# Weighting the edge one-hots on VectorE instead of GpSimd in a graph network kernel

## The chip, the cores and the metric

The kernel runs on one core of a Trainium2 chip. The metric is the device time of one execution in microseconds (us), from start to end, taken as the median of several executions. A profile of one execution gives, beside that, the span from the first to the last instruction and the start and length of every instruction.

## The reference

The program is a graph network on 1,250 nodes with 512 features. It first runs four layers of sparse attention and an MLP over 21,250 edges, then one last layer that sums neighbours with edge weights:

```python
scores = jnp.einsum('ehd,ehd->eh', q[src], k[dst])
...
out = jax.ops.segment_sum(attn[:, :, None] * v[dst], src, num_segments=N)
...
msgs = x[col] * vals[:, None]
agg = jax.ops.segment_sum(msgs, row, num_segments=n)
```

The kernel turns both sparse steps into dense ones. For that it needs two 1,250 x 1,250 tables: how many edges lead from node s to node d (the attention uses its logarithm), and the sum of the weights of those edges (the last layer multiplies by it).

## The kernel before

The work has three stages on the one core: the tables are built, then four layers run, then the last layer. The change touches the first stage alone.

**How the tables are built.** The edges are sorted by destination and cut into 56 groups of 384 (`GK` = 3 blocks of 128 edges each). A group's destinations lie within a window of `WIN` = 28 columns. For each group, TensorE multiplies the one-hots of the sources (`onehot`, 128 edges x 1280 nodes, bf16, one for each block) with a small operand `win` (128 edges x 4 x 28, bf16). The first of the four parts of `win` is the one-hot of the destination column in the window; the other three are that one-hot times the three bf16 parts of the edge's weight (`wpart`), which together hold the weight in full. The sums land in PSUM, and VectorE adds them into the tables `CW` in SBUF.

**Who does what in a group.** TensorE: 30 matmuls (L1464). VectorE: four additions into `CW` (L1060, L1062, L1064, L1067), of which the three on the weight table are a chain that must keep its order, and two of the source one-hots for the group three ahead (`sources`, L1028); for one group in eight it makes all three. ScalarE makes the third source one-hot of the other seven groups (L708, L770).

**The windows.** `win` is made for four groups at a time, a *chunk* (`CHUNK_G` = 4, so 14 chunks), in two alternating buffers. VectorE compares the column offsets (`window`, L1022: one TENSOR_TENSOR of 128 x 336 elements), and GpSimd then multiplies the result three times (L599: three TENSOR_TENSOR of 128 x 336 elements in a chunk). TensorE waits for `e_parts` before the first group of a chunk.

**Order.** The groups are run in blocks of eight (`groups(i)`, seven blocks). `j` is the group in the block. `window(1, ...)` stands at the end of group j = 0 and serves the groups j = 4 to 7 of the same block; `window(0, ...)` stands at the end of j = 4 and serves the next block. TensorE starts group n when VectorE has ended the chain of additions of group n - 2 (`e_chain`). Between blocks VectorE has other work (angles, remainders of the layers' rows, first statistics), and between chosen groups TensorE, ScalarE and GpSimd have some too (`between`). When the last group is added, VectorE sets `tables_done` (L1134), for which the other engines wait. All of this stands inside blocks that are entered when a flag says that the windows hold, which they do for these inputs.

## Time and profile before

| what | value |
|---|---|
| median of 3 runs | 1897.14 us (1895.46 to 1897.63) |
| profiled execution, its own time | 1893.53 us |
| span of that execution | 1891.7 us |
| granted TensorE clock, mean | 0.990 of full speed |
| TensorE busy over the span | 1765.5 us (93%) |
| VectorE busy | 1273.4 us (67%) |
| ScalarE busy | 915.1 us (48%) |
| GpSimd busy | 362.1 us (19%) |

The shares are averages over all stages. In the first 190 us, where the tables are built, the picture is another one than in the layers, and it has to be read by itself. In the rows of the trace, PE is TensorE, DVE is VectorE, ACT is ScalarE and POOL is GpSimd. The length of a VectorE instruction is from its start to its last write; the next one can start before that, so the distance between two starts tells what an instruction takes of the engine.

### The profile page before, as it was taken

How to read it: one execution, taken by the hardware profiler on the slowest of the kernel's cores; microseconds unless marked ns; L12 is line 12 of the kernel's file. 1: busy time of each engine (PE TensorE's matmuls, PEld its weight loads, DVE VectorE, ACT ScalarE, POOL GpSimd, SP SyncE). 2: the span in 40 equal slices, each digit the busy share in tenths (PEclk: the TensorE clock that was granted, in tenths of full speed). 3: DMA queues.
4: the chain of work that ended last, by engine and by line, in shares of the span. 5: the costliest groups of instructions: out<-in, count | busy, mean ns of one | idle time of the engine just before them, and what ended most of it. 6: DMA issues, size and time to landing. Idle time of an engine off the chain costs nothing.

```text
span 1891.7 us, 30938 instructions
## 1 busy us (share of the span) xinstructions
PE 1765.5 (93%) x11881; PEld 1510.1 (80%) x11881; DVE 1273.4 (67%) x2425; ACT 915.1 (48%) x1472; POOL 362.1 (19%) x482
## 2 busy tenths in 40 slices
PE   4755799999999999999999999999999999999898
PEld 3655588888887888888888888888878888888777
DVE  8999955766866566667655766767556667575744
ACT  8796744544542345445523544545325445453221
POOL 3222330000252200000532000004420000034201
PEclk9899999999999999999999999999999999999999
DMA  3040652422310223223200422323003223241121
GB/s 126 2 128 2 259 190 75 140 93 86 128 57 16 70 94 126 88 93 115 84 27 27 137 93 88 126 88 100 23 16 126 88 93 128 86 143 50 41 80 70
DMA packets 63926, 170.31 MB, mean 90 GB/s; under 512 B 5977, under 2 KB 24186, under 8 KB 63773
## 3 DMA queue, kind: packets, MB, share of 16 engines
q10 hardware_dynamic: 23040, 102.41, 16.2%
q1 hardware_dynamic: 40740, 65.91, 10.7%
q8 instruction: 96, 1.57, 0.3%
q14 instruction: 50, 0.41, 0.1%
HBM read 146.58 MB, written 17.02 MB: 86 GB/s over the span
## 4 chain that ended last, share of the span: by engine, by line
PE 77%; DVE 13%; issue 5%; ACT 2%; DMA 1%; DVEq 1%; POOL 1%; SPq 0%; POOLq 0%; ACTq 0%
PE ps L1464 66%; PE ps L1681 9%; DVE onehot L1028 2%; PE ps L1601 1%; DVE prob L1220 1%; DVE PT_lo L1236 1%; DVE CW L1062 1%; DVE CW L1064 1%; DVE CW L1060 1%; DVE CW L1067 1%; ACT PT_hi L835 1%; DMA piece<-in_L_gnn_m_w_dram 1%; DVEq L1052 1%; PE ps L1896 1%; DMA stacks_sb<-b_stack 0%
## 5 line engine op out<-in xcount | busy, mean ns | idle before, releaser
L835 ACT ACTIVATE PT_hi<-ps 128x512 fp32r<-128x512 f32 x400 | 238.5, 596 | 245.3 <-PE ps L1681 244.5
L1236 DVE TENSOR_TENSOR PT_lo<-ps,PT_hi 128x512 fp32r<-128x512 f32 x400 | 274.2, 686 | 49.8 <-ACT PT_hi L835 42.3
L819 ACT ACTIVATE prob<-prob,nmax 128x1250 f32<-128x1250 f32 x160 | 214.0, 1338 | 138.9 <-DVE nmax L1220 138.9
L1681 PE MATMUL ps<-ident,prob 128*128 128x128 f32 x1600 | 248.4, 278 | 12.3 <-DVE PT_lo L1236 12.2
L1220 DVE CUSTOM_DVE_ANT_0 prob<-ps,Lr 128x1250 f32<-128x1250 f32 x160 | 232.2, 1451 | 33.6 <-PE ps L1464 31.9
L1681 PEld LDWEIGHTS ps<-ident,prob 128*128 128x128 f32 x1600 | 181.7, 140 | 79.2 <-DVE PT_lo L1236 61.4
L1464 PE MATMUL ps<-PT_hi,v_hi 128*128 128x256 f32 x800 | 228.0, 285 | 1.2 <-DVE PT_lo L1236 1.2
L1464 PE MATMUL ps<-PT_lo,v_hi 128*128 128x256 f32 x800 | 226.1, 283 | 0.0
L1464 PE MATMUL ps<-PT_hi,v_lo 128*128 128x256 f32 x800 | 225.9, 282 | 0.0
L1464 PE MATMUL ps<-yT,wqk_hi 128*128 128x512 f32 (+1 forms) x768 | 213.0, 364 | 4.3 <-DVE yT L1173 4.3
L1464 PE MATMUL ps<-k_hi,q_hi 128*128 128x512 f32 (+2 forms) x480 | 192.3, 401 | 1.1 <-DMA stacks_sb<-b_stack 0.5
L1464 PE MATMUL ps<-k_hi,q_lo 128*128 128x512 f32 (+2 forms) x480 | 170.1, 354 | 0.0
L1464 PE MATMUL ps<-k_lo,q_hi 128*128 128x512 f32 (+2 forms) x480 | 169.7, 353 | 0.0
L1464 PE MATMUL ps<-win,onehot 128*128 128x112 bf16 x1680 | 99.7, 222 | 68.3 <-DVE CW L1067 55.9
L1464 PEld LDWEIGHTS ps<-PT_hi,v_hi 128*128 128x128 f32 x800 | 152.5, 191 | 2.5 <-issue 2.0
L1464 PEld LDWEIGHTS ps<-PT_lo,v_hi 128*128 128x128 f32 x800 | 152.8, 191 | 0.1
L1464 PEld LDWEIGHTS ps<-win,onehot 128*128 128x128 bf16 x1680 | 92.3, 103 | 75.7 <-issue 65.0
L1464 PEld LDWEIGHTS ps<-PT_hi,v_lo 128*128 128x128 f32 x800 | 152.7, 191 | 0.0
L1464 PEld LDWEIGHTS ps<-yT,wqk_hi 128*128 128x128 f32 x768 | 132.1, 189 | 23.7 <-DVE yT L1173 4.8
L1250 DVE SCALAR_TENSOR_TENSOR x<-ps,rnorm,x 128x512 f32<-128x512 f32 x160 | 119.3, 746 | 46.5 <-PE ps L1464 46.5
L624 POOL TENSOR_TENSOR wo_lo<-piece,wo_hi 128x512 fp32r<-128x512 f32 x16 | 20.4, 1272 | 620.3 <-ACT wo_hi L866 620.3
L1464 PE MATMUL ps<-yT,wqk_lo 128*128 128x512 f32 (+1 forms) x384 | 137.2, 357 | 0.0
(200 smaller groups left out, 3695.8 us busy)
## 6 DMA issues: line engine op xcount, KB each, us to landing
Lr<-l_table ACTq DMA_DIRECT2D x160, 625.0 KB, 3.8
piece<-in_L_gnn_m_w_dram SPq DMA_DIRECT2D x32, 256.0 KB, 2.6
w_table<-CW SPq DMA_DIRECT2D x5, 1250.0 KB, 8.5
l_table<-CW SPq DMA_DIRECT2D x10, 625.0 KB, 3.1
prob<-w_table SPq DMA_DIRECT2D x10, 625.0 KB, 3.9
x<-in_x_dram SPq DMA_DIRECT2D x2, 2304.0 KB
CW<-CW SPq DMA_DIRECT2D x7, 625.0 KB
piece<-in_L_gnn_wo_dram SPq DMA_DIRECT2D x16, 256.0 KB, 2.6
```

Of the source, the lines that this page charges most:

```text
L624: pool.tensor_tensor(lo, raw, hi.bitcast(F32), ALU.subtract).then_inc(S["piece_split"], 1)
L819: act.activation(buf, buf, ACT.Exp, bias=nmax[:, i % 4:i % 4 + 1], scale=-1.0, accum_out=rsum[:, i % 4:i % 4 + 1]).then_inc(S["exped"], 1)
L835: act.activation(o, i, ACT.Copy).then_inc(S["pt_hi"], 1)
L1028: m = dve.tensor_scalar(onehot[:, j % SBUFS, b, :], iota_h[:], eT[:, 0, b, group], None, ALU.is_equal)
L1052: base = dve.value_load(grow_i[0:1, bass.ds(i * UNROLL_G + j, 1)], min_val=0, max_val=N - WIN)
L1060: dve.tensor_tensor(weights, weights, sums[:, 1], ALU.add).then_inc(e_chain, 1)
L1062: dve.tensor_tensor(counts, counts, sums[:, 0], ALU.add).then_inc(e_count, 1)
L1220: dve.tensor_tensor_reduce(prob[:, i % 3, 0:N], ps[:, off:off + N], Lr[:, i % LBUFS, 0:N], -SCALE, BIG, ALU.add, ALU.min, nmax[:, i % 4:i ...
L1236: dve.tensor_tensor(lo, i, hi.bitcast(F32), ALU.subtract).then_inc(S["pt_split"], 1)
L1250: dve.scalar_tensor_tensor(out=x[:, t, :], in0=bank(wo_bank(h, t)), scalar=rnorm[:, i % 8:i % 8 + 1], in1=x[:, t, :], op0=ALU.mult, op1=AL ...
L1464: return pe.matmul(o, a, b, start=start, stop=stop)
L1681: m = pe.transpose(bank(5 + n % 2, at * P, (at + 1) * P), prob[:, (NT * h + 2 * g + j) % 3, d * P:(d + 1) * P], ident[:])
```

## The change

GpSimd's loop over the chunks loses its three multiplications and their waits; the two small tasks between the chunks stay. VectorE gets a function `weigh(c)` with the same three multiplications. For chunk 0 it stands directly behind the comparison; for the others it stands in the group after the one that holds the comparison (j = 1 and j = 5), between the first source one-hot and the last addition. The comparison of a fifteenth chunk, which no group used, is left out.

```diff
             pool.wait_ge(eplan, 2)
-            flag = pool.value_load(grow_i[0:1, NG:NG + 1], min_val=0, max_val=1)
             for c in range(NCH):
-                with pool.If(flag < 1):
-                    pool.wait_ge(e_win, c + 1)
-                    for part in range(3):
-                        oh = win[:, c % 2, :, 0, :].rearrange("p (g b) w -> p g b w", b=GK)
-                        o = win[:, c % 2, :, 1 + part, :].rearrange("p (g b) w -> p g b w", b=GK)
-                        wp = wpart[:, part, c * CHUNK_G:(c + 1) * CHUNK_G, :]
-                        m = pool.tensor_tensor(o, oh, wp.unsqueeze(3).to_broadcast([P, CHUNK_G, GK, WIN]), ALU.mult)
-                    m.then_inc(e_parts, 1)
-                    pool.wait_ge(e_parts, c + 1)
                 for work in between.get(c, ()):
                     work()
...
+            def weigh(c):
+                dve.wait_ge(e_win, c + 1)
+                oh = win[:, c % 2, :, 0, :].rearrange("p (g b) w -> p g b w", b=GK)
+                for part in range(3):
+                    o = win[:, c % 2, :, 1 + part, :].rearrange("p (g b) w -> p g b w", b=GK)
+                    wp = wpart[:, part, c * CHUNK_G:(c + 1) * CHUNK_G, :]
+                    m = dve.tensor_tensor(o, oh, wp.unsqueeze(3).to_broadcast([P, CHUNK_G, GK, WIN]), ALU.mult)
+                m.then_inc(e_parts, 1)
...
                 window(0, slice(0, CHUNK_G))
+                weigh(0)
                 for j in range(AHEAD):
...
                     sources(j + AHEAD, 0, ahead)
+                    c = 2 * i + 1 + j // CHUNK_G
+                    if j % CHUNK_G == 1 and c < NCH:
+                        weigh(c)
                     dve.wait_ge(e_chain, at + 2)
...
-                    if j == CHUNK_G:
+                    if j == CHUNK_G and (i + 1) * UNROLL_G < NG:
                         window(0, bass.ds(i * UNROLL_G + UNROLL_G, CHUNK_G))
```

The order of the instructions shows where they go. VectorE at the start of the loop, before (the comparison of chunk 0, the seven source one-hots of groups 0 to 2, then the first group's additions):

```order
L1022 TENSOR_TENSOR win<-iota_h,eT 128x12x28
L1028 TENSOR_SCALAR onehot<-iota_h,eT 128x1280 x7
L1033 UNCONDITIONAL_BRANCH
L1105 COMPARE_AND_BRANCH
L1052 TENSOR_LOAD grow_i
```

and of the change:

```order
L1012 TENSOR_TENSOR win<-iota_h,eT 128x12x28
L1023 TENSOR_TENSOR win<-win,wpart 128x12x28 x3
L1027 TENSOR_SCALAR onehot<-iota_h,eT 128x1280 x7
L1032 UNCONDITIONAL_BRANCH
L1108 COMPARE_AND_BRANCH
```

The three multiplications now stand ahead of the one-hots of the first groups. VectorE in group 1, before (from the comparison of chunk 1 on, which ends group 0; `CW` are the tables):

```order
L1022 TENSOR_TENSOR win<-iota_h,eT 128x12x28
L1052 TENSOR_LOAD grow_i
L1052 ISA x2
L1060 ISA
L1060 TENSOR_TENSOR CW<-CW,ps 128x10x28
L1062 ISA
L1062 TENSOR_TENSOR CW<-CW,ps 128x10x28
L1064 TENSOR_TENSOR CW<-CW,ps 128x10x28
L1028 TENSOR_SCALAR onehot<-iota_h,eT 128x1280
L1067 TENSOR_TENSOR CW<-CW,ps 128x10x28
L1028 TENSOR_SCALAR onehot<-iota_h,eT 128x1280
```

and of the change:

```order
L1012 TENSOR_TENSOR win<-iota_h,eT 128x12x28
L1052 TENSOR_LOAD grow_i
L1052 ISA x2
L1060 ISA
L1060 TENSOR_TENSOR CW<-CW,ps 128x10x28
L1062 ISA
L1062 TENSOR_TENSOR CW<-CW,ps 128x10x28
L1064 TENSOR_TENSOR CW<-CW,ps 128x10x28
L1027 TENSOR_SCALAR onehot<-iota_h,eT 128x1280
L1023 TENSOR_TENSOR win<-win,wpart 128x12x28 x3
L1070 TENSOR_TENSOR CW<-CW,ps 128x10x28
L1027 TENSOR_SCALAR onehot<-iota_h,eT 128x1280
```

Three more instructions stand between the first one-hot and the last addition of the group. This pattern comes 13 times.

## Rows read from the trace of the kernel before

**Rows 1.** Stretches: start:end us, length, busy us (count) by engine, clock, DMA.

```profile
100.00:163.50 63.50, 38.24 (x702) 35.26 (x703) 63.50 (x154) 60.23 (x52) 15.04 (x19) 1.00 0.34 96
163.50:190.00 26.50, 13.79 (x211) 12.79 (x211) 24.81 (x63) 8.78 (x9) 6.45 (x15) 0.86 0.01 2
190.00:1891.70 1701.70, 1654.88 (x10128) 1409.41 (x10128) 1094.63 (x2008) 762.65 (x1341) 312.71 (x400) 1.00 0.28 93
```

**Rows 2.** Waits of VectorE, 14 to 190 us: total us, times, longest.

```profile
DVE CW L1060 <- PE ps L1464: 4.8, 2, 2.7
DVE CW L1060 <- issue: 2.2, 6, 0.7
```

**Rows 3.** Groups by line, 0 to 420 us: busy us, mean ns | idle before.

```profile
L1028 DVE TENSOR_SCALAR onehot<-iota_h,eT 128x1280 bf16<-128x1280 f16 x126 | 74.9, 603 | 0.0
L1022 DVE TENSOR_TENSOR win<-iota_h,eT 128x336 bf16<-128x336 f16 x15 | 7.4, 495 | 1.6 <-issue 1.6
...
L599 POOL TENSOR_TENSOR win<-win,wpart 128x336 bf16<-128x336 bf16 x42 | 34.2, 842 | 126.3 <-DVE win L1022 126.3
```

**Rows 4.** Timeline of VectorE, 123 to 130 us: start, length.

```profile
123.77 0.49 DVE L1022 TENSOR_TENSOR win<-iota_h,eT 128x336 bf16<-128x336 f16 x1
124.19 0.43 DVE L1060 TENSOR_TENSOR CW<-CW,ps 128x280 f32 x1
...
125.26 0.89 DVE L1028 TENSOR_SCALAR onehot<-iota_h,eT 128x1280 bf16<-128x1280 f16 x1
126.07 0.43 DVE L1067 TENSOR_TENSOR CW<-CW,ps 128x280 f32 x1
...
127.02 0.43 DVE L1060 TENSOR_TENSOR CW<-CW,ps 128x280 f32 x1
...
128.09 0.54 DVE L1028 TENSOR_SCALAR onehot<-iota_h,eT 128x1280 bf16<-128x1280 f16 x1
128.55 0.43 DVE L1067 TENSOR_TENSOR CW<-CW,ps 128x280 f32 x1
...
129.37 0.43 DVE L1060 TENSOR_TENSOR CW<-CW,ps 128x280 f32 x1
```

**Rows 5.** Timeline of the start of the loop.

```profile
14.81 0.51 DVE L1022 TENSOR_TENSOR win<-iota_h,eT 128x336 bf16<-128x336 f16 x1 [1.62 <-issue]
15.24 4.79 DVE L1028 TENSOR_SCALAR onehot<-iota_h,eT 128x1280 bf16<-128x1280 f16 x7
15.41 2.89 POOL L599 TENSOR_TENSOR win<-win,wpart 128x336 bf16<-128x336 bf16 x3 [6.45 <-DVE win L1022]
...
18.36 5.00 PE L1464 MATMUL ps<-win,onehot 128*128 128x112 bf16 x60 [8.56 <-POOL win L599]
...
22.15 0.45 DVE L1060 TENSOR_TENSOR CW<-CW,ps 128x280 f32 x1 [2.11 <-PE ps L1464]
```

**Rows 6.** Timeline around VectorE's longest wait.

```profile
73.36 0.39 PE L1464 MATMUL ps<-f_w,hcond 16*128 16x16 f32 x2
...
78.75 5.49 PE L1464 MATMUL ps<-win,onehot 128*128 128x112 bf16 x60
...
79.13 0.68 DVE L1028 TENSOR_SCALAR onehot<-iota_h,eT 128x1280 bf16<-128x1280 f16 x1
...
82.51 0.45 DVE L1060 TENSOR_TENSOR CW<-CW,ps 128x280 f32 x1 [2.70 <-PE ps L1464]
```

**Rows 7.** Timeline of VectorE around a long operation on two SBUF inputs.

```profile
98.15 2.27 DVE L1093 TENSOR_TENSOR row_raw<-row_raw,row_part 71x2048 f32<-71x2048 f32 x1
100.36 0.43 DVE L1060 TENSOR_TENSOR CW<-CW,ps 128x280 f32 x1
```

**Rows 8.** Timeline of TensorE: groups of 30 matmuls after idle time of several lengths.

```profile
52.42 2.96 PE L1464 MATMUL ps<-win,onehot 128*128 128x112 bf16 x30 [7.69 <-DVE CW L1067]
...
102.57 1.64 PE L1464 MATMUL ps<-win,onehot 128*128 128x112 bf16 x30 [2.91 <-DVE CW L1067]
...
170.53 2.96 PE L1464 MATMUL ps<-win,onehot 128*128 128x112 bf16 x30 [5.47 <-DVE CW L1067]
```

## The prediction

> **What bounds the kernel now.** The page's average points to TensorE, but the change lies in one stage, so I read the stages first. From 100 to 163.5 us, VectorE is busy for 63.50 of 63.50 us, with TensorE at 38.24 and GpSimd at 15.04 [rows 1]. The reader is to see a stage in which VectorE has no gap at all. Then I looked at what VectorE waits for while the tables are built: 4.8 us in two waits for TensorE, and 2.2 us in six short ones after a branch or a register load [rows 2]. The rest of some 175 us is work. So a microsecond added to VectorE here is a microsecond on the kernel, except where it falls into one of those waits, and the end of this stage (`tables_done`) is what the layers start from. From 190 us on TensorE is busy for 1654.88 of 1701.70 us [rows 1], and nothing of the change stands there; the layers only start later or earlier. GpSimd, on the other hand, spent 126.3 us waiting for the comparison [rows 3]. Its 34.2 us of multiplying are off the path, but the timeline shows that they are not free for others.
>
> **What GpSimd's multiplications cost VectorE today.** A group without them takes 129.37 - 127.02 = 2.35 us from first addition to first addition. The group in which GpSimd multiplies takes 127.02 - 124.19 = 2.83 us [rows 4]. The excess of 0.48 us sits in the source one-hots: one takes 126.07 - 125.26 = 0.81 us of the engine where an undisturbed one takes 128.55 - 128.09 = 0.46 us, and the rest is in the next one. The additions, which have an input in PSUM, keep their length. So each chunk gets 0.48 us back when GpSimd falls silent. The mean of the one-hots, 603 ns against an undisturbed 540, over 126 of them is 7.9 us [rows 3, 4], which is 13 times 0.48 and the start's share.
>
> **What a multiplication costs on VectorE.** The trace has none of this form there. The nearest row is the comparison: the same 128 x 336 elements into the same `win`, with an innermost-broadcast second input just as the weights have. It takes 124.19 - 123.77 = 0.42 us of the engine [rows 4]. It differs in one thing: its second input is f32, while all three operands of the multiplication are bf16. Could that make it faster? From 336 elements in 0.42 us and 2048 elements in 100.36 - 98.15 = 2.21 us [rows 7] an element takes 1.046 ns, and what is fixed is 0.07 us. With two elements handled at a time it would be 0.07 + 168 x 0.001046 = 0.245 us; that is my lower bound. The upper one is 0.49 us, the comparison's whole length, if each multiplication had to drain before the next one. I take 0.42, since the row it is nearest to has the same shape and the same broadcast. This choice is the weakest step of the sum.
>
> The Trainium skill, "VectorE: DVE Perf Modes", section "The perf-mode tier table", gives a `tensor_tensor` with bf16 operands in SBUF two elements per cycle; by that the multiplication would take my lower bound and the kernel 1899.0 us. The Trainium skill, "Vector Engine (DVE) Microarchitecture Reference", section "5.1 Performance modes", asks for an innermost step of plus or minus one on every operand, and reports 1x where one operand of two-byte data is a single element read again and again, as the weight is here 28 times; by that it stays at 0.42 us and the sum below stands. The comparison is no test of either, because of its f32 input, and no row here shows the case.
>
> **The sum.** With m for a multiplication:
>
> 1. Thirteen chunks in the loop, each 3m - 0.48 us. With m = 0.42: 1.26 - 0.48 = +0.78 us. The three instructions stand ahead of the last addition, whose chain TensorE waits for. TensorE's next group then starts later, but it needs 1.64 us [rows 8], and VectorE has a one-hot and a further whole group (2.35 us) to do before it needs that result, so TensorE does not become the one waited for. ScalarE's one-hots get more room.
> 2. One of the thirteen is covered. In group 17, VectorE waits 2.70 us for TensorE at 82.51 us [rows 6], because TensorE does the small matmuls of the conditioning from 73.36 us to 78.75 us, between two groups. What started them lies ahead of chunk 5's multiplications, and these fall into the VectorE group that ends at 79.13 + 0.68 = 79.81 us, right ahead of the wait. So twelve count: 12 x 0.78 = +9.4 us. If that cover were gone, +0.8 us more. At two of the six short waits, up to 0.27 us each might be filled as well; I leave them at nothing.
> 3. The unused fifteenth comparison goes: -0.42 us.
> 4. The start. Today TensorE's first group starts at 18.36 us, released by GpSimd, which multiplied from 15.41 us for 2.89 us [rows 5]. Afterwards: the comparison is written at 14.81 + 0.51 = 15.32 us, three multiplications end their time on the engine at 15.36 + 1.26 = 16.62 us, and the three one-hots of group 0 are written at 16.62 + 2 x 0.46 + 0.54 = 18.08 us. That is 0.27 us earlier. The first seven one-hots in sum took 4.79 us under GpSimd [rows 5] and will take 6 x 0.46 + 0.54 = 3.3 us, so VectorE is done at 19.9 us and still waits for TensorE until about 21.9 us: -0.27 us.
> 5. GpSimd's remaining tasks (a remainder of the conditioning, a memset, a copy) are no longer queued behind multiplications and come a little earlier. Nobody waits for them: VectorE's 63.50 of 63.50 us says that the statistics' input had landed. Nothing for it. The DMA queue is passed by nothing.
>
> Sum: 9.4 - 0.42 - 0.27 = +8.7 us. The profiled execution took 1893.53 us, of which its span of 1891.7 us is all but 1.8 us that the change does not touch. It would become 1902.2 us. That execution lies 3.6 us below the median of the runs, 1897.14 us, so against the median I expect 1897.1 + 8.7 = 1905.8 us, 0.46% more. I round down to 1905.5 us for the short waits that may be filled.
>
> In terms of m the sum is 12 x (3m - 0.48) - 0.42 + (3m - 1.53) = 39m - 7.7 us. It crosses zero at m = 0.20 us, and it reaches 0.2% (3.8 us, about what a measurement of this kernel can tell from no change) at m = 0.29 us.
>
> **Rivals.**
>
> *The multiplications run two elements at a time.* m = 0.245 us, sum +1.9 us: 1899.0 us, no change that can be told. For it: all three operands are bf16 and VectorE's one-hots show that packed modes exist, with 1280 elements in 0.46 us. Against it: the broadcast innermost dimension. This is the tier table's rule of the Trainium skill. Chance 0.12.
>
> *TensorE's clock drops in the loop.* After 7.69 and 5.47 us of idle time a group takes 2.96 us instead of 1.64 [rows 8], and the granted clock of the stretch with the second is 0.86 [rows 1], so it was at 1.2 instead of 2.4 GHz for a part of it. After 2.91 us it still takes 1.64 us. The longest new gap is that between the ends of two chains with a comparison and the multiplications between them, less the matmuls: 0.42 + 2.35 + 1.26 - 1.64 = 2.39 us, which is below 2.91. But the mean load falls too, and VectorE would wait for TensorE. If the clock drops in each block, groups take 2.96 us against VectorE's 2.35, and some 0.6 us per group is lost for perhaps one group a block: +4 us, 1910 us. Chance 0.07.
>
> *The multiplications take their whole length.* m = 0.49 us: 39 x 0.49 - 7.7 = +11.4 us, 1908.5 us. For it would speak a stall on the fresh write of the one before; against it, the additions in chain on the same table do not show it. Chance 0.06.
>
> *Faster than before.* It needs m below 0.20 us at three a chunk, or more than 1.26 us of relief per chunk, where the groups beside each other show 0.48. The start shows that GpSimd can cost more: 4.79 against 3.3 us for seven one-hots [rows 5]. If each chunk had a cost like that 1.5 us somewhere, the change would gain 3 us. In the middle of the loop no row shows it. Chance 0.03.
>
> **How the numbers follow.** The forecast has 0.72, with its own range 1903.5 to 1907.5 us for the spread of the runs and the short waits. Adding the cases at 1908.5 and 1910 at the top and the near side of the packed case takes the range to 1901.5 to 1910 us, which leaves out most of the packed case, the gain, and a remainder. Slower by over 0.2%: 0.72 + 0.07 + 0.06 and a little of the packed case = 0.86. Within 0.2%: 0.11. Faster: 0.03.
>
> **What would show each step.** In the changed kernel's trace: three TENSOR_TENSOR on `win` with starts 0.42 us apart (0.25 would be the packed case, 0.49 the drained one); no one-hot over about 0.55 us; a group with the multiplications of 2.35 + 1.26 = 3.6 us; two such groups and one third one-hot in a block of eight, which grows by 2 x 0.78 us; the wait of 2.70 us down to about 1.9; the first group at 18.1 us; `tables_done` some 8.5 us later; the layers of the same length as before. The prediction is wrong if m is another, if VectorE begins to wait for TensorE in the loop, or if the layers change their length.

## The result and the profile after

The change makes the kernel slower, as forecast, but by 12.4 and 14.4 us in two comparisons, where the sum had 8.7 us.

| | before | after |
|---|---|---|
| first comparison, median | 1896.43 us (1895.46 to 1897.63, 4 runs) | 1908.79 us (1906.33 to 1910.73, 4 runs) |
| ratio, 95% interval | | 1.0062 (1.0047 to 1.0077) |
| the same two kernels, second comparison | 1895.51 us (21 runs) | 1909.91 us (1904.5 to 1912.47, 5 runs) |
| ratio, 95% interval | | 1.0075 (1.0062 to 1.0089) |
| span of the profiled execution | 1891.7 us | 1908.9 us, in the second comparison 1902.7 us |
| granted TensorE clock, mean of that span | 0.990 | 0.981, in the second comparison 0.985 |

The predicted time was 1905.5 us with a range of 1901.5 to 1910 us. Both medians of the change lie in the range, 3.3 and 4.4 us above the predicted time, and both lie above 1903.5 to 1907.5 us, the range that the forecast without its rivals had. The two profiled executions of the same changed kernel lie 6.2 us apart, one being the slowest of its four runs and the other the fastest of its five. That difference turns out to be the most useful thing in the data, so both are read below.

First, one chunk on VectorE in the middle of the loop, from the comparison on (timeline of VectorE in the changed kernel; start, length). It answers to [rows 4].

```profile
134.09 0.50 DVE L1012 TENSOR_TENSOR win<-iota_h,eT 128x336 bf16<-128x336 f16 x1
134.51 0.44 DVE L1060 TENSOR_TENSOR CW<-CW,ps 128x280 f32 x1
...
135.58 0.54 DVE L1027 TENSOR_SCALAR onehot<-iota_h,eT 128x1280 bf16<-128x1280 f16 x1
136.04 1.33 DVE L1023 TENSOR_TENSOR win<-win,wpart 128x336 bf16<-128x336 bf16 x3
137.30 0.43 DVE L1070 TENSOR_TENSOR CW<-CW,ps 128x280 f32 x1
137.66 0.54 DVE L1027 TENSOR_SCALAR onehot<-iota_h,eT 128x1280 bf16<-128x1280 f16 x1
138.12 0.43 DVE L1060 TENSOR_TENSOR CW<-CW,ps 128x280 f32 x1
```

The three multiplications take 137.30 - 136.04 = 1.26 us, so m = 0.42 us, the value chosen. The group takes 138.12 - 134.51 = 3.61 us, and the one-hot ahead of them is at its undisturbed 0.54 us instead of 0.89.

The start of the loop (timeline of the changed kernel), which answers to [rows 5]:

```profile
15.35 1.35 DVE L1023 TENSOR_TENSOR win<-win,wpart 128x336 bf16<-128x336 bf16 x3
16.61 3.32 DVE L1027 TENSOR_SCALAR onehot<-iota_h,eT 128x1280 bf16<-128x1280 f16 x7
...
21.96 0.45 DVE L1060 TENSOR_TENSOR CW<-CW,ps 128x280 f32 x1 [2.02 <-PE ps L1467]
```

The seven one-hots take 3.32 us (3.3 was forecast), and the first addition starts 0.19 us earlier than before (0.27 was forecast).

Now the two lines that the sum of work does not explain. VectorE's waits while the tables are built (total us, times, longest), in the first execution of the changed kernel, and then in the second. They answer to [rows 2], where the total was 7.0 us.

```profile
DVE CW L1060 <- PE ps L1467: 9.5, 6, 2.7
DVE CW L1060 <- issue: 3.6, 5, 1.5
```

```profile
DVE CW L1060 <- PE ps L1467: 3.6, 3, 2.0
DVE CW L1060 <- issue: 3.1, 4, 1.5
```

That is 13.1 us in one execution and 6.7 us in the other. `tables_done` is set at 206.14 and at 199.62 us (timeline of VectorE, first and then second execution):

```profile
206.14 0.06 DVE L1137 MEMSET viol<- 1x1 f32 x1
```

```profile
199.62 0.06 DVE L1137 MEMSET viol<- 1x1 f32 x1
```

Before, it was (timeline of VectorE, kernel before):

```profile
189.80 0.06 DVE L1134 MEMSET viol<- 1x1 f32 x1
```

The executions are 6.52 us apart there, and their waits are 13.1 - 6.7 = 6.4 us apart. In other words, VectorE did the same work in both, and what differs is how long it stood still for TensorE. Taken against before, the work alone grew by 16.34 - (13.1 - 7.0) = 10.2 us in the one, and by 9.82 - (6.7 - 7.0) = 10.1 us in the other. The prediction had 9.5 us of work, of which 0.8 us would lie in a wait.

Why VectorE waits is seen on TensorE (timeline of TensorE, first execution: start, busy time, count, in brackets the idle time before and what ended it):

```profile
101.00 4.82 PE L1467 MATMUL ps<-win,onehot 128*128 128x112 bf16 x60 [2.39 <-DVE CW L1070]
...
111.35 2.88 PE L1467 MATMUL ps<-win,onehot 128*128 128x112 bf16 x30 [2.87 <-DVE CW L1070]
...
137.99 4.84 PE L1467 MATMUL ps<-win,onehot 128*128 128x112 bf16 x60 [2.39 <-DVE CW L1070]
...
149.87 1.63 PE L1467 MATMUL ps<-win,onehot 128*128 128x112 bf16 x30 [2.39 <-DVE CW L1070]
```

The gap of 2.39 us stands there exactly as worked out ahead. What was not forecast is what follows it: two groups take 4.82 us, when twice 1.64 us is 3.28, and after the gap of 2.87 us one takes 2.88 us. A group at 1.2 GHz throughout took 2.96 us [rows 8], so TensorE ran at 1.2 GHz for part of these. After other gaps of 2.39 us, as at 149.87, the clock stays up.

But most of what the first execution waited longer than before stands elsewhere, behind the gap of 7.7 us in which VectorE computes the angles, between the first two blocks of eight. Before, that gap was as long (7.69 us); one group took 2.96 us behind it [rows 8], and in the next one the clock came back (timeline of TensorE, kernel before):

```profile
55.53 2.07 PE L1464 MATMUL ps<-win,onehot 128*128 128x112 bf16 x30 [0.16 <-issue]
```

In the first execution of the changed kernel (timeline of TensorE):

```profile
54.83 2.96 PE L1467 MATMUL ps<-win,onehot 128*128 128x112 bf16 x30 [7.68 <-DVE CW L1070]
58.85 2.96 PE L1467 MATMUL ps<-win,onehot 128*128 128x112 bf16 x30 [1.06 <-DVE CW L1070]
...
63.99 4.57 PE L1467 MATMUL ps<-win,onehot 128*128 128x112 bf16 x60
```

and in the second:

```profile
53.98 2.96 PE L1467 MATMUL ps<-win,onehot 128*128 128x112 bf16 x30 [7.72 <-DVE CW L1070]
57.97 1.64 PE L1467 MATMUL ps<-win,onehot 128*128 128x112 bf16 x30 [1.04 <-DVE CW L1070]
```

Ahead of this second group TensorE now stands idle for 1.06 us instead of 0.16, because the chain that it waits for now has the multiplications in it. In the one execution the granted clock stays at 0.50 from 54.9 to 64 us, in the other it is 1.00 from 58 us on; why, no run shows. By stretches (start:end, length, busy us of TensorE, its weight loads, VectorE, ScalarE and GpSimd, clock, DMA), first execution:

```profile
100.00:163.50 63.50, 39.41 (x640) 36.35 (x640) 62.33 (x153) 55.01 (x47) 0.91 (x2) 0.91 0.34 96
206.20:1908.90 1702.70, 1658.12 (x10128) 1412.30 (x10128) 1093.27 (x2009) 763.41 (x1341) 312.85 (x400) 0.99 0.28 93
```

In the first stretch the clock was 1.00 and VectorE had no gap [rows 1]; now the clock is 0.91, VectorE stands still for 1.17 us (mostly in two waits of 0.55 and 0.50 us behind the slow groups at 101.00 and 137.99, which the trace puts down to issue, as a register load stands between the wait and the addition), and GpSimd's 15.04 us have become 0.91. The layers take 1702.7 us instead of 1701.7 [rows 1]. The extra time therefore arises before them, all but about 1 us.

The three longest waits behind that start (timeline of VectorE, first execution; the last one is the wait behind the conditioning and answers to [rows 6]):

```profile
62.59 0.45 DVE L1060 TENSOR_TENSOR CW<-CW,ps 128x280 f32 x1 [1.03 <-PE ps L1467]
...
67.76 0.45 DVE L1060 TENSOR_TENSOR CW<-CW,ps 128x280 f32 x1 [2.73 <-PE ps L1467]
...
90.05 0.45 DVE L1060 TENSOR_TENSOR CW<-CW,ps 128x280 f32 x1 [2.09 <-PE ps L1467]
```

The wait that was 2.70 us is 2.09 us (some 1.9 was forecast), and 0.84 us in the second execution. So it did shrink, as the cover of one chunk asks, but in the second by more than a chunk; the small matmuls of the conditioning ran at the high clock throughout there. The waits at 62.59 and 67.76 us belong to the groups just shown, and neither is in the second execution: together 3.8 of the 6.4 us between the two, with another 1.25 us behind the conditioning. The waits behind gaps of 2.2 to 2.4 us are 0.88, 0.55, 0.50 and 0.77 us in the first execution (2.7 us in all) and 0.55 and 0.73 us in the second. A wait of 1.54 us in the last block, behind a gap of 5.47 us, is in both. Every one of these waits stands behind groups that took more than 1.64 us, none behind a group that was only late.

### The profile page after: what moved, and what is told of

It reads as the page before. It is cut to its first block, busy times and chain, and to the rows that moved or that the text cites. A ratio compares the mean times of both kernels' runs of the same rounds, so it can differ in the third digit from the quotient of the medians.

```text
span 1908.9 us, 30907 instructions
## 1 busy us (share of the span) xinstructions
PE 1779.2 (93%) x11881; PEld 1522.6 (80%) x11881; DVE 1282.0 (67%) x2466; ACT 916.3 (48%) x1472; POOL 327.9 (17%) x440
## 3 DMA queue, kind: packets, MB, share of 16 engines
q1 hardware_dynamic: 40740, 65.91, 10.6%
## 4 chain that ended last, share of the span: by engine, by line
PE 79%; DVE 12%; issue 5%; ACT 2%; DVEq 1%; POOL 1%; DMA 1%; POOLq 0%; ACTq 0%
PE ps L1467 68%; PE ps L1684 9%; DVE onehot L1027 2%; PE ps L1604 1%; DVE prob L1223 1%; DVE PT_lo L1239 1%; DVE CW L1062 1%; DVE CW L1064 1%; DVE CW L1060 1%; DVE CW L1070 1%; DVE win L1023 1%; ACT PT_hi L825 1%; DMA piece<-in_L_gnn_m_w_dram 1%; PE ps L1899 1%; DVEq L1052 0%
## 5 line engine op out<-in xcount | busy, mean ns | idle before, releaser
L1467 PE MATMUL ps<-win,onehot 128*128 128x112 bf16 x1680 | 108.9, 234 | 74.2 <-DVE CW L1070 56.8
L1467 PEld LDWEIGHTS ps<-win,onehot 128*128 128x128 bf16 x1680 | 101.7, 110 | 81.6 <-issue 81.6
```

The source lines that it names most:

```text
L1467: return pe.matmul(o, a, b, start=start, stop=stop)
```

## The experiments

The theories to tell apart: (work) the time is work on VectorE, 39m - 7.7 us, with m = 0.42; (clock) on top of it, TensorE's longer gaps let its clock fall, and VectorE waits for it; (placement) what is on top of it comes from the multiplications standing inside the chain of additions, or from late one-hots of ScalarE; (GpSimd) its multiplications cost VectorE another amount than 0.48 us a chunk. The expectations of the first four experiments call the clock theory A and placement B. Each comparison has its own runs of the kernel before: 1895.93 us (16 runs) for the first four, 1895.51 (21 runs) for the next four, and 1893.97 (9 runs) for the last two. So the ratios and the differences are what to compare.

| run | median, us | over before, us | ratio (95%) | `tables_done`, us | VectorE's waits, us | from `tables_done` to the end, us |
|---|---|---|---|---|---|---|
| change, first | 1908.79 | +12.4 | 1.0062 (1.0047 to 1.0077) | 206.14 | 13.1 | 1702.8 |
| change, again | 1909.91 | +14.4 | 1.0075 (1.0062 to 1.0089) | 199.62 | 6.7 | 1703.1 |
| spread | 1905.39 | +9.5 | 1.0054 (1.0040 to 1.0067) | 198.09 | 5.7 | 1701.4 |
| filled | 1907.13 | +11.2 | 1.0055 (1.0042 to 1.0069) | 201.50 | 9.1 | 1704.4 |
| no multiplications | 1889.66 | -6.3 | 0.9968 (0.9956 to 0.9980) | 184.94 | 8.5 | 1705.3 |
| before, filled | 1895.96 | 0.0 | 1.0002 (0.9993 to 1.0011) | 190.36 | 7.5 | 1703.7 |
| pairs | 1898.96 | +3.5 | 1.0011 (1.0002 to 1.0020) | 192.91 | 7.6 | 1706.2 |
| pairs, spread | 1898.43 | +2.9 | 1.0010 (1.0001 to 1.0020) | 191.82 | 6.8 | 1704.3 |
| GpSimd too | 1926.64 | +31.1 | 1.0154 (1.0140 to 1.0167) | 219.95 | 12.7 | 1704.9 |
| behind | 1904.58 | +10.6 | 1.0053 (1.0040 to 1.0067) | 201.79 | 9.6 | 1702.0 |
| filled near | 1906.13 | +12.2 | 1.0070 (1.0056 to 1.0084) | 200.30 | 7.8 | 1703.5 |

The last three columns are of one profiled execution each, the others of all runs. Of before they are 189.80, 7.0 and 1701.9 us. The change again, the spread and the near filled kernel were profiled in their fastest run; the change at first, no multiplications, pairs and behind in their slowest. So a difference of medians can't be read off these columns. The last one differs by up to 4.8 us between kernels that are alike there; what sets it was not tried.

### The multiplications spread over the groups

```diff
+PARTS_AT = {1: (0,), 2: (1, 2), 5: (0, 1), 6: (2,)}
...
-                    if j % CHUNK_G == 1 and c < NCH:
-                        weigh(c)
+                    if j in PARTS_AT and c < NCH:
+                        weigh(c, PARTS_AT[j])
```

> The changed kernel with the same 42 multiplications on VectorE, but not three in one group: one in the group after the comparison and two in the next (the other way round for every second chunk). The work on VectorE is the same. Theory A (beside the work itself, the longer gaps between TensorE's groups let its clock fall, and VectorE then waits for TensorE): the longest regular gap falls from 2.39 us to about 2, most of the waits of VectorE for TensorE inside the loop go, the granted clock of 100 to 176 us rises from 0.91 towards 1.00, and the time falls by 2 to 4 us against the changed kernel, to 1905 to 1907 us. Rival B (the excess over the sum comes from the multiplications standing in the chain or from late ScalarE one-hots, and the clock is a mere sign of it): no change, 1908 to 1910 us, since as many multiplications stand ahead of a last addition.

The same work in smaller pieces. It measured +9.5 us, where the change has +12.4 and +14.4 in its two comparisons. `tables_done` comes 8.29 us after that of before, the forecast being about 8.5, though this is its fastest run. In the same stretch of the loop (by stretches, this kernel):

```profile
100.00:163.50 63.50, 37.29 (x662) 34.34 (x659) 62.97 (x155) 53.82 (x46) 0.90 (x2) 0.97 0.35 96
```

The clock is 0.97 where the two executions of the change have 0.91 and 0.92. Over the longer stretch that the expectation names, 100 to 176 us, it is only 0.93, where they have 0.91 and 0.93, since two places behind 163.5 us are slow here. So the time came out nearly at the sum of the work, as the clock theory has it and placement has not, but the clock itself rose less than expected. The interval just overlaps with that of the repeated change (1.0067 against 1.0062), so the gain of 3 to 5 us is likely, not certain, by the times alone. A shorter gap is no full cure either (timeline of TensorE, this kernel):

```profile
95.17 2.90 PE L1470 MATMUL ps<-win,onehot 128*128 128x112 bf16 x30 [1.97 <-DVE CW L1073]
```

### Unread matmuls in TensorE's gaps

```diff
+FILL = {n: 10 for n in (*range(2, 12), *range(18, 29), *range(36, 56))}
+FILL.update({10: 100, 26: 30, 50: 80})
...
                     c, gl = divmod(n, CHUNK_G)
+                    for _ in range(FILL.get(n, 0)):
+                        mm(bank(6, 0, 4 * WIN), ident_b[:], ident_b[:, 0:4 * WIN], True, True)
```

(Two waits are added too, so that the identity and the PSUM bank are free.)

> The changed kernel, with matmuls on TensorE whose result nobody reads: 10 of 112 columns ahead of most groups' waits, and 100, 30 and 80 ahead of the three groups that follow VectorE's other work. VectorE, ScalarE and GpSimd are as in the changed kernel. Theory A (the clock): the granted clock stays at 1.00 nearly everywhere, VectorE's waits for TensorE in the loop shrink from 13 us to under 4, and what is left is the work: 1896.4 + 8.5 less the old waits that also go, so 1902 to 1905 us. Rival B (placement or ScalarE): 1908 us or more, because TensorE only gets more to do.

This missed: +11.2 us, with waits of 9.1 us where under 4 were expected. The clock of the loop did come back (0.97 from 100 to 163.5 us), but the wait behind the conditioning grew. Ahead of group 18 (timeline of TensorE, then of VectorE, this kernel):

```profile
77.83 0.37 PE L1470 MATMUL ps<-f_w,hcond 16*128 16x16 f32 x2
...
78.36 0.58 PE L1470 MATMUL ps<-f_w,hcond 16*128 16x16 f32 x2
...
82.72 1.11 PE L1470 MATMUL ps<-ident_b 128*128 128x112 bf16 x10
83.62 3.01 PE L1470 MATMUL ps<-win,onehot 128*128 128x112 bf16 x30
```

```profile
87.41 0.45 DVE L1063 TENSOR_TENSOR CW<-CW,ps 128x280 f32 x1 [4.17 <-PE ps L1470]
```

The wait was 2.09 and 0.84 us in the change and is 4.17 us here. The ten unread matmuls in front of the group account for 0.9 us of it. The rest is the conditioning itself: the granted clock is 1.00 up to about 78.1 us and 0.50 from there on, and its small matmuls take 6.7 us (from 76.02 to 82.72 us). In the change the same matmuls took 5.6 us in the first execution, where the clock fell late, and 4.6 us in the second, where it did not fall; before, they took 5.4 us. Why the clock falls there sooner or later no run shows. So the wait behind the conditioning moves by itself, and this run is no clean test of the clock theory.

### No multiplications at all

```diff
-                for part in range(3):
...
-                    m = dve.tensor_tensor(o, oh, wp.unsqueeze(3).to_broadcast([P, CHUNK_G, GK, WIN]), ALU.mult)
-                m.then_inc(e_parts, 1)
+                dve.sem_inc(e_parts, 1)
```

> The changed kernel without the three multiplications on any engine: the weight parts of win are zero throughout, so the weight table is left out. Both GpSimd's interference and VectorE's new work are gone. Prediction's step (GpSimd costs VectorE 0.48 us per chunk today): against before, -12 x 0.48 - 0.42 - 1.5 (first group at 16.8 us) = -7.7 us, 1888.7 us. If GpSimd's interference costs nothing on the path, only -2 us, 1894.5 us. Against the changed kernel, theory A expects 39 x 0.42 = 16 us of work plus the 4 us of clock: -20 us.

It gains 6.3 us over the kernel before. The forecast's constant is 7.7 us: 12 x 0.48 for GpSimd's multiplications in the loop, 0.42 for the comparison, and 1.53 for the start. The start was not tested, because the edit takes it back: the zeros are written by GpSimd, VectorE waits for them, and its first comparison starts at 16.17 us instead of 14.81 (timeline of this kernel):

```profile
16.17 0.51 DVE L1014 TENSOR_TENSOR win<-iota_h,eT 128x336 bf16<-128x336 f16 x1 [1.63 <-issue]
...
22.18 0.45 DVE L1057 TENSOR_TENSOR CW<-CW,ps 128x280 f32 x1 [2.02 <-PE ps L1464]
```

Its first addition comes 0.03 us after that of before [rows 5]. Without the start the forecast is 5.8 + 0.4 = 6.2 us, and 6.3 were measured. So the 0.48 us a chunk hold over the whole loop, within the scatter of the runs.

### The kernel before with the same fill

```diff
+FILL = {n: 10 for n in (*range(2, 12), *range(18, 29), *range(36, 56))}
```

(The same edit as above, on the kernel before.)

> The kernel before, with the same unread matmuls as in the run above it. Theory A: before, VectorE waited 7.0 us in all, of which some 2 to 3 us hang on groups at the low clock, so 1893.5 to 1895 us. Rival B: no gain, 1896 us or more. If the matmuls themselves delay groups, slower than before.

No change, 1.0002, although the mean clock rises to 0.992; the gain of 1 to 2 us that the clock theory asked for did not come. The clock is not what limits the kernel before: it is at 1.00 in the loop anyway.

### The change again

The changed kernel without an edit, beside the next three.

> The changed kernel once more, beside the runs that are compared with it, since its difference to the spread version is near the scatter of the runs. Expected by all theories: 1907 to 1910 us, 11 to 14 us over before, granted clock of the whole span 0.980 to 0.983.

Its five runs go with the clock theory: one took 1904.5 us at a mean clock of 0.985; the other four took 1909.5 to 1912.5 us at 0.979 to 0.981.

### Weights stored in pairs

```diff
+            for part in range(3):
+                m = dve.tensor_copy(wtwice[part][:], wpart[:, part].unsqueeze(3).to_broadcast([P, NG, GK, 2]))
...
-                    m = dve.tensor_tensor(o, oh, wp.unsqueeze(3).to_broadcast([P, CHUNK_G, GK, WIN]), ALU.mult)
+                    m = dve.tensor_tensor(o, oh, wp.unsqueeze(2).to_broadcast([P, CHUNK_G * GK, WIN // 2, 2]), ALU.mult)
```

Each weight stands twice side by side, so that the innermost step of every operand is one and the broadcast is a level further out.

> The changed kernel, but each part of a weight is stored twice side by side (three copies of 336 elements at the start), so that the innermost dimension of the multiplication is a pair with step 1 instead of one element read 28 times. Same result. If the broadcast is what keeps the multiplications at one element at a time: starts 0.245 us apart instead of 0.42, so -39 x 0.175 = -6.8 us, and +1.3 us for the copies: some 5.5 us less, 1903 us, and less still if the shorter gaps spare the clock (1900 us). If the all-bf16 operands already had all the speed there is (or VectorE does not pack such an operation at all): starts stay 0.42 us apart, and the time rises by 1.3 us.

+3.5 us instead of +14.4: the branch of the broadcast came true, and the time fell twice as far as its 5.5 us. A chunk (timeline of VectorE, this kernel):

```profile
128.69 0.81 DVE L1030 TENSOR_TENSOR win<-win,wtwice 128x336 bf16<-128x336 bf16 x3
129.42 0.44 DVE L1077 TENSOR_TENSOR CW<-CW,ps 128x280 f32 x1
```

Three take 0.73 us, 0.243 us each. The lower bound of the prediction, worked out as half the elements and the same fixed part, was 0.245 us. So this form can run two elements at a time, and what kept it from that in the change is the innermost broadcast. The Trainium skill, "Vector Engine (DVE) Microarchitecture Reference", section "5.1 Performance modes", says as much for a single two-byte element read over and over in an operation on two sources, and for a repeated row it gives the packed mode; both rows agree with it.

The copies turned out to cost nothing. They fill an idle time of VectorE, and the first comparison starts at 14.84 us where it started at 14.83 (timeline of VectorE, this kernel):

```profile
13.25 0.82 DVE L1013 COPY wtwice<-wpart 128x336 bf16<-128x336 bf16 x3
14.84 0.51 DVE L1018 TENSOR_TENSOR win<-iota_h,eT 128x336 bf16<-128x336 f16 x1 [0.77 <-issue]
```

The time fell by more than the work. By the sum it is 39 x (0.42 - 0.243) = 6.9 us less; measured were 11.0 us less. That the rest is waits on a slow TensorE again is likely, but not shown: the two profiled executions stood still for about as long (7.6 and 6.7 us). What the trace does show is the loop (timeline of TensorE, this kernel, all of whose groups from 113 to 165 us take 1.64 us):

```profile
130.11 1.64 PE L1474 MATMUL ps<-win,onehot 128*128 128x112 bf16 x30 [1.87 <-DVE CW L1077]
...
140.66 1.64 PE L1474 MATMUL ps<-win,onehot 128*128 128x112 bf16 x30 [1.87 <-DVE CW L1077]
```

With shorter multiplications the regular gap is 1.87 us and no longer 2.39 (0.42 + 2.35 + 0.73 - 1.64 = 1.86), and not one group behind it in this stretch is slow. The slow place of the loop is at 104.00 us, where a group takes 2.96 us behind 2.92 us of idle time; before, one took 1.64 us behind 2.91 [rows 8].

### Pairs, and spread

Both edits together.

> Both edits at once, the weights stored in pairs and the multiplications spread over two groups: the lowest cost of the multiplications on VectorE that was found. By the sum with m = 0.245: before + 1.9 + 1.3 = 1899.5 us, with the longest regular gap of TensorE under 1.7 us and so hardly a drop of the clock. If before stays faster than this, GpSimd is the better place for this kernel. Under 1896 us it would be a better kernel than before.

+2.9 us against +3.5: no difference that can be told. From 100 to 163.5 us its clock is 1.00, and VectorE is busy for all of the 63.50 us, as before the change. With no slow group left in the loop the time is 1.1 us over the sum of the work, 39 x 0.243 - 7.7 = +1.8 us. It is the best of the versions with the multiplications on VectorE, and the kernel before is still faster by 0.1%, which is hardly clear of the scatter.

### GpSimd multiplies as well

```diff
+                    pool.wait_ge(e_win, c + 1)
+                    for part in range(3):
+                        oh = ident_b[:, 0:WIN].unsqueeze(1).unsqueeze(1).to_broadcast([P, CHUNK_G, GK, WIN])
...
+                        m = pool.tensor_tensor(scratch[part][:], oh, wp.unsqueeze(3).to_broadcast([P, CHUNK_G, GK, WIN]), ALU.mult)
```

The changed kernel, in which GpSimd also does three multiplications a chunk, on other tensors and into a scratch that nobody reads.

> The changed kernel, and GpSimd multiplies as before as well, from other tensors into a scratch of its own that nobody reads. VectorE's work is as in the changed kernel, so the run prices GpSimd's interference by itself. The prediction's step: two one-hots of a group stretched by 0.35 and 0.13 us, so +0.48 us a chunk, +5.8 us in twelve chunks, and up to 1.4 us at the start: 1914 to 1916 us. If a multiplication of VectorE, with two inputs in SBUF, is held up by GpSimd too: more, up to 2 us a chunk, 1930 us. If the interference costs nothing on the path: 1909 us.

A miss, on the high side: +31.1 us, 16.7 us above the change. Timeline of VectorE and GpSimd in one chunk, this kernel:

```profile
130.77 2.41 POOL L602 TENSOR_TENSOR scratch<-ident_b,wpart 128x336 bf16<-128x336 bf16 x3 [10.84 <-DVE win L1025]
130.97 0.44 DVE L1075 TENSOR_TENSOR CW<-CW,ps 128x280 f32 x1
131.32 0.44 DVE L1077 TENSOR_TENSOR CW<-CW,ps 128x280 f32 x1
131.68 0.89 DVE L1040 TENSOR_SCALAR onehot<-iota_h,eT 128x1280 bf16<-128x1280 f16 x1
132.50 1.89 DVE L1036 TENSOR_TENSOR win<-win,wpart 128x336 bf16<-128x336 bf16 x3
134.31 0.43 DVE L1083 TENSOR_TENSOR CW<-CW,ps 128x280 f32 x1
```

The additions keep their 0.44 us under GpSimd; the one-hot takes 0.82 us of the engine instead of 0.46; and the three multiplications take 134.31 - 132.50 = 1.81 us instead of 1.26. So GpSimd costs 0.36 + 0.55 = 0.91 us a chunk here and not 0.48. The groups by line (busy us, mean ns; this kernel):

```profile
L1040 DVE TENSOR_SCALAR onehot<-iota_h,eT 128x1280 bf16<-128x1280 f16 x126 | 72.9, 586 | 0.0
...
L1036 DVE TENSOR_TENSOR win<-win,wpart 128x336 bf16<-128x336 bf16 x42 | 27.4, 704 | 0.0
```

Against 544 and 498 ns in the change, that is 126 x 42 ns = 5.3 us and 42 x 206 ns = 8.7 us, together 14.0 us. `tables_done` is 20.3 us later than in the repeated change, of which 12.7 - 6.7 = 6.0 us are waits. That adds up. The expectation had only counted the one-hots. The Trainium skill, "SBUF — State Buffer", section "SBUF: two separate sides", names both kinds as sharing a port pair with GpSimd: VectorE's two-port modes, and instructions with two inputs in SBUF when GpSimd reads SBUF. The rows agree: the multiplication with two inputs in SBUF and the one-hot are held up, the additions with an input in PSUM are not. That the one-hot runs in a two-port mode no row names.

### The multiplications at the end of the group

```diff
-                    c = 2 * i + 1 + j // CHUNK_G
-                    if j % CHUNK_G == 1 and c < NCH:
-                        weigh(c)
...
                     if j == CHUNK_G and (i + 1) * UNROLL_G < NG:
                         window(0, bass.ds(i * UNROLL_G + UNROLL_G, CHUNK_G))
+                    c = 2 * i + 1 + j // CHUNK_G
+                    if j % CHUNK_G == 1 and c < NCH:
+                        weigh(c)
```

> The kernel of the change, with the three multiplications of a chunk moved from the middle of group j = 1 and 5 to its end, behind the last addition and the last source one-hot. The work is the same; only the longest gap of TensorE between two groups shrinks from 0.42 + 2.35 + 1.26 - 1.64 = 2.39 us to 2.35 + 1.26 - 1.64 = 1.97 us, twice a block of eight. If the length of that single gap decides whether TensorE's clock stays up, the waits of VectorE for TensorE go as in the kernel with the spread multiplications (longest gap 1.55 us): 1905 us, about 9 us over before, and VectorE's waits by 206 us near 6 us. If what counts is the clumping of VectorE's work over a whole block of eight and not the one gap, nothing changes: 1908 to 1910 us, waits of 7 to 13 us. If TensorE's groups being late behind an interrupted chain were the cost, it would also go to 1905 us.

The time, +10.6 us and 1.0053, is nearest to what the first theory asked for (about +9), but the waits are 9.6 us and not 6, and its premise was wrong (timeline of TensorE, this kernel):

```profile
126.43 4.73 PE L1467 MATMUL ps<-win,onehot 128*128 128x112 bf16 x60 [2.42 <-DVE CW L1067]
138.43 1.64 PE L1467 MATMUL ps<-win,onehot 128*128 128x112 bf16 x30 [1.97 <-DVE CW L1067]
```

One of the two gaps in a block is 1.97 us and the other 2.42, since the third one-hot of 0.46 us fell into it. From 100 to 165 us all three long gaps lead into a slow group, and none of the three short ones does. Outside that stretch it is not so neat: behind the short gap ahead of 30.57 us two groups take 4.81 us, and behind a long one at 173.18 us a group takes 1.63 us. The clock of the stretch is 0.92, as in the change, so by this run alone the interrupted chain is not ruled out as a part of the cost.

### Unread matmuls in the long gaps alone

```diff
+FILL = {n: 20 for n in (3, 7, 11, 19, 23, 27, 39, 43, 47, 51)}
```

(The loop over these numbers and the two added waits are as in the filled kernel above.)

> The kernel of the change, with 20 matmuls on the identity, whose result nobody reads, ahead of ten of the groups that wait longest for a chain (3, 7, 11, 19, 23, 27, 39, 43, 47 and 51). They take about 1.1 us at full clock and 2 us at the low one, within the 2.39 us gap, and there are none in the stretches where the earlier filled kernel lost time at the low clock. If idle TensorE time in those gaps is what lets the clock fall, the groups behind the gaps take 1.64 us again, VectorE's waits for TensorE fall to the 2 to 4 us of the conditioning, and the time is 1904 to 1906 us. If the clock falls for another reason, the time stays at 1908 to 1910 us, or rises by up to 2 us where the unread matmuls run at the low clock.

The trace does what the clock theory expects in the loop: the clock from 100 to 163.5 us is 0.97 instead of 0.91, and VectorE's waits there are down to a single one of 0.56 us. But the time is +12.2 us, 1.0070, and does not tell itself from the change. A good part stands again behind the conditioning (timeline of VectorE, this kernel):

```profile
86.86 0.45 DVE L1062 TENSOR_TENSOR CW<-CW,ps 128x280 f32 x1 [2.99 <-PE ps L1469]
```

That is 0.9 and 2.15 us more than in the two executions of the change. Here no unread matmul stands ahead of the group waited for; the conditioning took 6.5 us (from 76.66 to 83.15 us), as its clock fell early again. In the profiled execution 1703.5 us pass after `tables_done`, 1.6 us more than before the change. The rest stays open, and with two missed forecasts the filling does not prove the clock theory.

## Why the prediction was right, and where it was short

**The number** was right with some luck. The forecast's own range, 1903.5 to 1907.5 us, missed both medians; they lie in the stated one because the rivals at 1908.5 and 1910 us had widened its top. Taken as an increase over 1897.1 us the range ends at +12.9 us, which holds the +12.4 us of the first comparison and not the +14.4 us of the second. The direction, and the size of the added work, came out by the mechanism that was named.

**What bounds the stage** (right). A microsecond put on VectorE there was a microsecond of the kernel: work grew by 10.1 to 10.2 us, with 9.5 forecast, and `tables_done` moved with it.

**The price m = 0.42 us** (right), called the weakest step. The two rivals on it are out: the rows have 0.42 us, not 0.245 and not 0.49. The pairs kernel shows why the packed rival failed: not the types, but the innermost broadcast. By the Trainium skill, "VectorE: DVE Perf Modes", section "The perf-mode tier table", m would have been 0.245 us; the measurement decides for 0.42 in this form. The rival with 0.49 us has 1908.5 us, which is nearly the measured time, and is wrong all the same.

**What GpSimd costs VectorE** (right for the kernel before). Without the multiplications the kernel gained 6.3 us, where 12 x 0.48 + 0.42 = 6.2. The two groups beside each other in [rows 4] priced it well, but only for the instructions that VectorE then had: with the multiplications on VectorE too, the same GpSimd work costs 0.91 us a chunk.

**The cover and the start** (right). The 2.70 us wait shrank to 2.09 and 0.84 us, and the start gave 0.19 us. That wait moves by more than the 0.8 us in question with TensorE's clock in the conditioning (it is 3.96 us in the kernel "behind"), so how much of a chunk it covers differs from run to run.

**TensorE does not become the one waited for** (wrong; this is the step that failed). Its sentence reasons that TensorE needs 1.64 us, and VectorE has more than that to do. The gap of 2.39 us was right, but 1.64 us is only true at the high clock; in the first execution VectorE waited 9.5 us for TensorE, against 4.8 before. The rival on the clock was argued down because 2.39 us is below the 2.91 us after which a group still took 1.64 [rows 8]. That compared one gap, which stands alone among gaps of at most 1.5 us between 90 and 165 us, with one that now comes twice a block, and in the changed kernel the same length goes both ways. It gave the rival 0.07 and +4 us; the measured excess over the sum of 8.7 us is 3.7 and 5.7 us. So the chance was far too low. That the size of +4 us came out was in part luck: it was reckoned as one slow group in each block behind the 2.39 us gaps, where the traces have 2.7 and 1.3 us of waits. In the first execution more than that, 3.8 us, stood behind the 7.7 us gap, which was there before, and where the multiplications only made TensorE idle once more while its clock was low. Of that place the prediction says nothing.

How sure that cause is: the slow groups behind the gaps, the granted clock, and the agreement of waits and time between two executions of one kernel are shown. That shorter gaps lessen it is supported by four kernels: spread lies 0.8 us over its sum and behind 1.9, and pairs and pairs spread took 3.5 and 2.9 us where their sum is 39 x 0.243 - 7.7 = 1.8. That filling the gaps cures it is not shown: both filled kernels kept the clock up in the loop and stayed 2.5 and 3.5 us above the sum. In their profiled executions 2.5 and 1.6 us more than before pass after `tables_done`, and both had a conditioning at the low clock for most of its length (waits of 4.17 and 2.99 us). Whether the filling has to do with that, or their other runs had it too, is not known. How the 3.7 and 5.7 us of the two medians divide into waits and layers is not known either, since only the slowest run of the one comparison and the fastest of the other were profiled.

## What to carry to other kernels

Work moved to the engine that bounds a stage costs its full length, less what its old place took from that engine; price both from neighbouring groups with and without it, and do it again for the instructions that will be there afterwards. Then look at what the engine that waits will do: a stretch that leaves TensorE idle a little longer, regularly, can cost a second time through its clock, so try the added work in small pieces rather than in one (here 3 to 5 us, likely and not certain). And give a broadcast operand of two-byte data a pair of copies innermost before moving it to VectorE: three copies, which fell into an idle time, took each of 42 multiplications from 0.42 to 0.243 us.

## What the runs showed of the hardware

- TensorE's clock after a gap is not a matter of that gap alone. In one kernel, groups behind 2.39 us of idle time took 1.64 us in some places and ran partly at 1.2 GHz in others (4.82 us for two), and in two executions of that kernel not always in the same places. Behind the regular gaps of 1.87 us of the pairs kernel no group was slow from 113 to 165 us; in the spread kernel one behind 1.97 us took 2.90 us.
- The runs of the changed kernel spread from 1904.5 to 1912.5 us (5 runs), those of the kernel before beside them from 1893.92 to 1898.28 us (21 runs). The fastest of the five has the highest mean clock, 0.985 against 0.979 to 0.981.
- Under steady small matmuls the granted clock fell too, from 1.00 to 0.50, and not at the same place: the conditioning took 4.6 us in one execution of the change, 5.6 us in the other, 5.4 us before and 6.7 us in the filled kernel.
- After 7.7 us of idle time TensorE's next group ran at the low clock (2.96 us) in both executions of the change; and behind a further gap of 1.06 and 1.04 us the group after it took 2.96 us in one and 1.64 us in the other.
- A VectorE multiplication with both inputs in SBUF is delayed by a GpSimd multiplication beside it: 0.60 us instead of 0.42 each. A source one-hot takes 0.82 us instead of 0.46, and an addition with an input in PSUM keeps its 0.44 us.
- A VectorE multiplication of 128 x 336 bf16 elements took 0.42 us with one element of the second input read 28 times, and 0.243 us with each element stored as a pair.
